# Local attention with half-row scores, softmax scaling on GpSimd and the output product inside the loop

## What is computed

```
q = rmsnorm(rope(x @ wq.T))                      # 16 heads of 64
k, v = x @ wkv.T                                 # one head of 64; k = rmsnorm(rope(k))
mask = (cols <= rows) & (rows - cols <= 128)
scores = einsum('bqgtd,bqgsd->bqgts', q, k) / sqrt(64)
attn = softmax(where(mask, scores, -1e30), axis=-1)
out = einsum('bqgts,bqgsd->bqgtd', attn, v)
return out @ wo.T
```

## Time and profile before

| | us |
|---|---|
| median of 3 runs | 1287.92 (1287.57 to 1290.64) |
| profiled execution | 1287.03 |
| its span, first to last instruction | 1285.2 |

### The profile page before, as it was taken

One profiled execution on the slowest core, in us unless ns is written; L12 is line 12 of the kernel. 1 busy time (PEld: TensorE's weight loads), 2 busy tenths in 40 slices (PEclk: granted clock), 3 DMA queues, 4 the chain that ended last, 5 costly groups with the idle time before them and its releaser, 6 DMA issues. The chain is left out here.

```text
span 1285.2 us, 18795 instructions
## 1 busy us (share of the span) xinstructions
PE 884.1 (69%) x6390; PEld 553.7 (43%) x6398; DVE 817.0 (64%) x2212; ACT 472.8 (37%) x1623; POOL 159.5 (12%) x116
## 2 busy tenths in 40 slices
PE   4476998675769995767699867766999679230630
PEld 4133665444336654453266534632666337020530
DVE  1387886754778866546788756466988464650236
ACT  0024775132237762322377622312777223000200
POOL 0042000000420000003300000024000000007145
PEclk9888999797889997887899978977999789755765
DMA  7033000000330000002400000024000000300112
GB/s 224 33 63 132 2 1 2 1 1 3 59 136 2 2 2 1 1 3 48 147 2 2 2 1 1 3 39 126 31 2 1 1 1 13 87 3 26 66 43 44
DMA packets 51381, 43.40 MB, mean 34 GB/s; under 512 B 46452, under 2 KB 47892, under 8 KB 50356
## 3 DMA queue, kind: packets, MB, share of 16 engines
q1 hardware_dynamic: 49222, 39.91, 10.6%
q0 software_dynamic: 2048, 2.10, 0.7%
HBM read 29.21 MB, written 4.72 MB: 26 GB/s over the span
## 5 line engine op out<-in xcount | busy, mean ns | idle before, releaser
L697 ACT ACTIVATE work<-ps,small,rq 128x160 f32<-128x160 f32 x512 | 241.0, 480 | 135.7 <-DVE small L660 135.7
L594 PE MATMUL ps<-kT,big 128*128 128x320 f32 x512 | 187.4, 473 | 0.0
L655 DVE TENSOR_REDUCE small<-ps 128x2 f32<-128x320 f32 x256 | 113.7, 486 | 50.9 <-PE ps L594 48.4
L260 PE MATMUL ps<-xT,s_proj_w 64*128 64x512 f32 x384 | 122.9, 772 | 27.0 <-DVE xb L534 14.3
L669 DVE TENSOR_SCALAR work<-work,small 128x128 f32<-128x128 f32 x512 | 112.0, 282 | 5.2 <-DVE small L665 0.8
L625 PE MATMUL ps<-turned,vwin 128*64 128x128 f32 x1024 | 84.2, 283 | 27.1 <-ACT big L712 23.1
L697 ACT ACTIVATION_READ_ACCUMULATOR work<-ps,small,rq 128x1 f32 x512 | 101.9, 199 | 0.0
L594 PEld LDWEIGHTS ps<-kT,big 128*128 128x128 f32 x512 | 83.0, 201 | 25.1 <-issue 25.1
L679 DVE COPY turned<-ps 128x512 f32<-128x512 f32 x128 | 87.6, 685 | 2.4 <-PE ps L606 2.4
L260 PEld LDWEIGHTS ps<-xT,s_proj_w 64*128 64x128 f32 x384 | 45.8, 244 | 89.7 <-issue 61.5
L565 POOL TENSOR_TENSOR big<-xb 128x1024 f32<-128x1024 f32 x32 | 75.7, 2376 | 59.1 <-DVE xb L534 59.1
(11 more groups left out here) (238 smaller groups left out, 1409.2 us busy)
## 6 DMA issues: line engine op xcount, KB each, us to landing
xb<-in_x SPq DMA_DIRECT2D x5, 4096.0 KB, 13.5
vrem<-xb SPq DMA_DIRECT2D x64, 64.0 KB, 2.1
s_proj_w<-in_proj_w SPq DMA_DIRECT2D x1, 1536.0 KB, 6.3
sent_rows<-zeros SPq DMA_DIRECT2D x8, 160.0 KB, 3.9
big<-sent_rows SPq DMA_DIRECT2D x5, 256.0 KB, 4.0
answered_rows<-big SPq DMA_DIRECT2D x8, 160.0 KB, 1.8
xb<-in_ffn_w SPq DMA_DIRECT2D x1, 1028.0 KB, 4.9
out<-vrem SPq DMA_DIRECT2D x8, 128.0 KB, 2.0
```

Of the source, the lines that this page charges most:

```text
L260: ins = nc.tensor.matmul(bank[banks + w][:], proj_w[half_rows(w), cols], xT[half_rows(w), :], start=True, stop=True)
L594: ins = nc.tensor.matmul(tiles, qT[:, c, 4 * hh:4 * hh + 4, :].rearrange("p a t -> p (a t)"), kT[:, :, CHUNK * c:CHUNK * c + SPAN], start= ...
L655: ins = v.tensor_reduce(small[:, c % 4, 0, 2 * e:2 * e + 2], s_bank(c, e)[:, 0:2 * SPAN].rearrange("p (a k) -> p a k", a=2), X, ALU.max)
L697: nc.scalar.activation(probs[:, c % 3, q, :], s_bank(c, q // 2)[:, SPAN * (q % 2):SPAN * (q % 2) + SPAN], ACT.Exp, bias=small[:, c % 4, 1, ...
```

## The change

In `project` and the setup: `kT` is stored once, 128 partitions by 1152, and made by one instruction. Mask and its row selector are loaded twice, for partitions 0 and 64 on, so that they too can be used by half rows.

In `windowed`:

- Scores: for each half of the heads and each of the two half rows, one product of 64 rows and 160 columns. The two heads of a pair now go to different banks.
- One maximum over both banks, 128 x 4 x 160, written into PSUM (`row_max`).
- The reciprocal alone stays on VectorE. A new GpSimd list multiplies `probs` (128 x 4 x 128) and `own` (128 x 4 x 32) by it, with the reciprocals as an operand broadcast along the keys.
- All five transposes go to banks 4 and 5, which are no longer doubled, and VectorE copies them in one instruction of 640 elements into a tile `pT` of its own. ScalarE's copy L706 is gone.
- The value products go to banks 6 and 7; ScalarE copies them in one instruction.
- The output product is taken per tile of 128 queries (four chunks), eight 128 x 64 products into a corner of bank 5 (`out_product`), ahead of the transposes of chunks 7, 11, ... 31; VectorE adds each to `h` (`add_out`). The last tile's follows the loop. The product of all tiles, its copy and its turning back are gone.
- Values of chunk n-3 instead of n-4 are taken in turn n, behind the transposes; on VectorE the copy of n-2 stands ahead of the reciprocal of n-1.

```diff
+                    for e in range(2):
...
+                        nc.tensor.matmul(masked, row_of_t[half_rows(e)], mask, start=True, stop=True,
+                                         skip_group_check=True)
                     for hh in range(2):
...
+                        for e in range(2):
+                            ins = nc.tensor.matmul(tiles[e][:, hh, :],
+                                                   qT[half_rows(e), c, 4 * hh:4 * hh + 4, :].rearrange("p a t -> p (a t)"),
+                                                   kT[half_rows(e), CHUNK * c:CHUNK * c + SPAN], start=False, stop=True,
+                                                   skip_group_check=True)
                     ins.then_inc(S["scores_done"], 1)
+
+                def out_product(i):
+                    pe.wait_ge(S["oT_ready"], NQ * (i + 1))
+                    for p in range(PAIRS):
+                        ins = nc.tensor.matmul(wo_at(i), oT[:, p, P * i:P * i + P], sbuf["wo0"][:, p, :], start=(p == 0),
+                                               stop=(p == PAIRS - 1), skip_group_check=True)
+                    return ins
 
                 def turn(c):
                     pe.wait_ge(S["scaled"], c + 1)
-                    if c >= 2:
-                        pe.wait_ge(S["pT_ready"], c - 1)
-                        pe.wait_ge(S["pTr_ready"], c - 1)
+                    if c >= 1:
+                        pe.wait_ge(S["pT_ready"], c)
+                    if added(c):
+                        out_product((c - 7) // 4)
                     for q in range(NQ):
-                        nc.tensor.transpose(bank[4 + c % 2][:, P * q:P * q + P], probs[:, c % 3, q, 0:P], ident[:])
-                    nc.tensor.transpose(bank[6 + c % 2][:, 0:P], own[:, c % 2, :],
-                                        ident[:]).then_inc(S["transposed"], 1)
+                        nc.tensor.transpose(bank[4][:, P * q:P * q + P], probs[:, c % 3, q, 0:P], ident[:])
+                    nc.tensor.transpose(bank[5][:, 0:P], own[:, c % 2, :], ident[:]).then_inc(S["transposed"], 1)
...
                 for n in range(CHUNKS + 2):
                     c = n
                     if c < CHUNKS:
                         v.wait_ge(S["scores_done"], c + 1)
...
+                        ch.step(v.tensor_reduce(row_max(c),
+                                                ps[:, s_banks(c), 0:2 * SPAN].rearrange("p e (h k) -> p e h k", h=2), X,
+                                                ALU.max))
...
                     c = n - 2
                     if c >= 0:
                         v.wait_ge(S["transposed"], c + 1)
                         if c >= 2:
                             v.wait_ge(S["pv_done"], c - 1)
-                        v.tensor_copy(pT[:, c % 2, :, :].rearrange("p q r -> p (q r)"),
-                                      bank[4 + c % 2][:]).then_inc(S["pT_ready"], 1)
+                        if added(c):
+                            add_out((c - 7) // 4)
+                        v.tensor_copy(pT[:, c % 2, :],
+                                      ps[:, 4:6, :].rearrange("p a n -> p (a n)")[:, 0:(NQ + 1) * P]).then_inc(
+                                          S["pT_ready"], 1)
+                    c = n - 1
+                    if 0 <= c < CHUNKS:
+                        v.wait_ge(S["exp_done"], NQ * (c + 1))
+                        v.reciprocal(small[:, c % 4, 3, :], small[:, c % 4, 2, :]).then_inc(S["sums_inverted"], 1)
...
+            @block.gpsimd
+            def _(g):
+                for c in range(CHUNKS):
+                    g.wait_ge(S["sums_inverted"], c + 1)
+                    if c >= 2:
+                        g.wait_ge(S["transposed"], c - 1)
+                    g.tensor_tensor(probs[:, c % 3, :, 0:P], probs[:, c % 3, :, 0:P], bc(small[:, c % 4, 3, :], P),
+                                    ALU.mult)
+                    g.tensor_tensor(own[:, c % 2, :].rearrange("p (q k) -> p q k", q=NQ), probs[:, c % 3, :, P:SPAN],
+                                    bc(small[:, c % 4, 3, :], CHUNK), ALU.mult).then_inc(S["scaled"], 1)
```

More of the change, by code:

```diff
@@ L91, in program @@
         shapes = {k: (list(v.shape), v.dtype) for k, v in inp.items()}
-        loaded = ["ident", "dft", "rope_cos", "rope_sin", "row_of_t", "window_mask", "lower", "first_weight",
+        loaded = ["ident", "dft", "rope_cos", "rope_sin", "lower", "first_weight",
                   "tok_w", "by_head", "wv0", "wo0", "router", "moe_b1", "moe_w2", "wvT1", "wl1", "proj_w"]
@@ L298, in _ @@
                     r = slice(D * half, D * half + D)
+                    for dst, src in ((row_of_t_rows, "row_of_t"), (window_mask_rows, "window_mask")):
+                        sp.dma_start(dst[D * half:D * half + CHUNK], inp[src]).then_inc(first_sem, 16)
+                        n += 1
                     for dst, src in ((qn, "q_norm"), (kn, "k_norm"), (bq, "bq1"), (bk, "bk1")):
@@ L334, in _ @@
                 v.tensor_tensor(both_halves[:], ident[:, 0:D], ident[:, D:P], ALU.add)
-                v.tensor_copy(row_of_t[0:CHUNK], sbuf["row_of_t"])
-                v.tensor_copy(window_mask[0:CHUNK], sbuf["window_mask"])
+                for half in range(2):
+                    r = slice(D * half, D * half + CHUNK)
+                    v.tensor_copy(row_of_t[r], row_of_t_rows[r])
+                    v.tensor_copy(window_mask[r], window_mask_rows[r])
                 v.tensor_scalar(bq[:], bq[:], 1.0 / D, None, ALU.mult)
@@ L576, in _, with s_banks, row_max, added @@
                 sp.wait_ge(S["x_loaded"], 16)
+            def s_banks(c):
+                return slice(2 * (c % 2), 2 * (c % 2) + 2)
+            def row_max(c):
+                return ps[:, s_banks(c), HALF - 2:HALF]
+            def added(c):
+                return c % 4 == 3 and c >= 7
+            def wo_at(i):
+                return bank[5][:, HALF - D * (1 + i % 2):HALF - D * (i % 2)]
             @block.tensor
```

141 lines of the change are left out of this document (49 added, 92 removed).

## The result

| | us |
|---|---|
| after, median of 4 runs | 1351.11 (1350.53 to 1355.14) |
| before, beside it on the same chip, median of 4 | 1288.57 (1287.57 to 1290.64) |
| ratio, 95% interval | 1.049 (1.0465 to 1.0515) |
| profiled execution after, its span | 1355.14, 1353.0 |

A forecast was written before the change was run, and what follows sets the result against it. A circle of copy, reciprocal, GpSimd scaling and transposes was to set 3.59 us per chunk against 3.17; with products, fill and drain +91 us, -5 and +1 outside the stage, on 1285.2: 1375 us, range 1320 to 1440.

The forecast's parts named there:

- the ring: In the local attention loop: copy, reciprocal, GpSimd's scaling and transposes wait for each other, one turn per chunk, 3.59 us.
- The scaling: GpSimd's two multiplications per chunk, taken at 1.69 us, the price of two full operands.
- the rival of a partly free broadcast: GpSimd's scaling pair takes 1.1 to 1.5 us; at 1.3 a chunk takes 3.20 and the total is 1325 us; 9%.
- the forecast's own condition: GpSimd's scaling pair takes 1.55 to 1.8 us per chunk; this case was given 70%.
- The release by GpSimd: Hand-over from GpSimd's scaling to the transposes, put at 0.12 us from a VectorE start after a GpSimd sum.
- fill: Start of each image's stage, up to the end of the first transposes, put at 7.9 us.
- The clock rival: In the loop, TensorE, idle a quarter of each chunk, falls to 1.2 GHz; half of the time, 1436 us; 12%.
- Outside the stage: Making kT in one instruction saves 1.3 us an image, -5 in all; two more setup loads cost +1 once.
- The longer circle: Exponentials, reciprocal, scaling, transposes, values, output copy: 6.3 us over two chunks, 3.15 each; next bound if the first were cut.

The follow-up runs named there:

- the run with both undone: Changed kernel with VectorE's reciprocal ahead of the copy and the output product back behind the loop: 1267.2 us, ratio 0.9845.
- the kernel with an add per chunk: Changed kernel with reciprocal ahead of the copy, output products spread as pairs in own columns, VectorE adding each pair to h: 1250.18 us, ratio 0.9711.

## Why the prediction was right, and by how much it was off

The direction and the mechanism held: the ring was named with its members in their order, and moving one of them (the reciprocal) dissolved it. The forecast was 1375 us, measured 1351. Term by term, for the ring:

| term | predicted | measured |
|---|---|---|
| transposes, first weights to last result | 0.76 | 164.41 to 165.18: 0.77 |
| to the copy | 0.04 | 165.18 to 165.22: 0.04 |
| copy until the reciprocal starts | 0.74 | 0.74 |
| reciprocal | 0.17 | 0.17 |
| release of GpSimd | 0.07 | 166.13 to 166.21: 0.08 |
| scaling, two instructions | 1.69 | 166.21 to 167.60: 1.39 |
| release of TensorE | 0.12 | 167.60 to 167.66: 0.06 |
| sum | 3.59 | 3.24 to 3.25 |

Two terms were mis-sized, and only these. **The scaling**: a broadcast second operand is cheaper than a full one (1.04 us against 1.27 for 512 elements, the run with the full operand), and the second instruction starts 0.05 before the first ends. By the mechanism this was the rival of a partly free broadcast (a pair of 1.1 to 1.5), to which I gave 9%, and its 1.3 was nearer than my 1.69; the forecast's own condition, 1.55 to 1.8, did not hold. I had taken the end whose rows were of the same operation, without a row for the operand's form. The estimate that the prediction drew from the Trainium skill's GPSIMD Engine Reference, section "Performance versus the Vector engine", 1.26 for the pair, was nearer too, though below the 1.39 measured. **The release by GpSimd**: 0.12 was VectorE's, TensorE needs 0.06.

For one stage: fill 7.7 (7.9 predicted); 31 turns with seven products 116.1 (125.7), of which the ring makes 10.9 less, six products at 1.93 and one at 4.11 make 15.7 (14.4); behind the last copy 8.3 (5.1). Sum 132.1 (138.7). The end was longer than predicted because the clock fell there, which the sum had left out: +2.1 in the last turn and +3.2 behind it (where the clock held, in the run with the reciprocal first, it took 5.2).

That 1351 is near 1375 is in part luck. The ring made the four stages 44 us shorter than the sum, which by itself would have come out nearer the rival's 1325; the lower clock at the ends of the images, about 20 us, and the part outside the stage, 8 us, gave over half of that back.

**The clock rival** was wrong where I had put it: in the loop TensorE stayed at the upper level (0.99). The rule of the page TensorE: Matmul & The Clock Gate in the Trainium skill, section "Part 4: PE-mode transpose", by which transposes do not count, is not borne out here either: the prediction had worked out that without them the loop would be loaded like the stretch that fell, and it did not fall. The rival came true where I had not looked, in the last chunks, where TensorE was busy 0.81 and 0.92 us in two stretches of 2 before it fell.

**Outside the stage** I had -4 us (kT as one instruction, the setup) and the span shows +4.2. kT is one instruction now and takes 1.28 us as predicted:

```profile
84.38 1.28 DVE L550 SCALAR_TENSOR_TENSOR kT<-xb,wqk,ps 128x1024 f32<-128x1024 f32 x1 [3.16 <-PE ps L449]
```

But the 1.3 us can't be seen behind it: from the last sum of an image to the next one's first scores it takes 144.3, 143.6 and 143.9 us, 143.4 to 144.9 before. The whole rest of the program, span less four stages, is 821.5 us before, 825.7 after, and 816.3 to 828.9 in the runs with the same instructions there as after. Whether the gain was lost to the clock in the projection or to something else stays open.

The longer circle, given as next at 3.15, was next indeed, at 2.90 (the run with both undone). Close behind it stands TensorE's own work: with the products spread it is 69.9 of 70 us busy at the same pace.

## What to carry to other kernels

Write down the order in which each engine takes its steps, and follow each wait to what stands queued behind it: here a 0.17 us instruction behind a waiting copy cost 65 us, some 20 of them through the clock at the ends of the images, and putting it ahead of that copy gave them back. A product that is put "inside" is free only where its engine waits anyway; ahead of the step that the others wait for it costs its full length. When one ring is opened, the next bound is near (3.24, then 2.90, with TensorE full at that pace), so size it before adding work.

## What the runs showed of the hardware that was not expected

- GpSimd: an elementwise product with a broadcast second operand took 1.04 us for 512 elements and 0.40 for 128, 1.67 ns an element; with two full operands 1.27 us for 512.
- VectorE and GpSimd: an add of 64 elements, both operands in SBUF, took 0.84 us beside GpSimd's scaling and ended with it; with one operand in PSUM 0.22. The Trainium skill's page SBUF — State Buffer, section "Who interferes with whom", says that a VectorE instruction with two SBUF inputs contends with a GpSimd one that reads SBUF, and that the second to issue blocks; these two runs agree.
- PSUM: a sum left open in a bank while other groups began there lost its earlier part, though their columns were apart; finished pairs in columns of their own did not. The Trainium skill's page PSUM — Partial Sum Buffer, section "The four PSUM rules", says so of two groups open at once in the same bank and the same 32 partitions: the second group's first product makes the first group's next one overwrite. The outputs of these runs agree; no trace shows the loss itself.
- TensorE's clock at the end of an image differed between images of one run: in the kernel with an add per chunk the first stage was 109.5 us and the others 103.3. What decides it there was not tested: in the kernel after it fell behind two stretches of 2 us with 0.81 and 0.92 us busy, and in the run with the reciprocal first it stayed at 1.00 through one with 0.42 busy (216 to 218).
